# First attention of a fused four-layer block: low parts by offsets, outputs one a step, twelve product buffers

## The chip, the cores and the metric

The program runs on one NeuronCore of one Trainium2 chip. The metric is the device time of one execution in microseconds (us), the median of three runs. TensorE (PE) multiplies matrices, VectorE (DVE) and GpSimd (POOL) work elementwise, ScalarE (ACT) evaluates functions, SyncE (SP) issues the transfers. The engines run their own instruction streams and meet at semaphores.

## The reference, cut to what matters

Eight stages follow each other (four attentions, four feed-forward layers), each of the form `x = x + stage(layernorm(x))` on x of 16 x 64 x 512. The change touches the first attention alone: for each of 8 heads of 8 channels, position t attends to a window of 16 neighbours.

```python
q = _pointwise(Wq, bq, x)
k = jnp.pad(_pointwise(Wk, bk, cond), ...)
v = jnp.pad(_pointwise(Wv, bv, cond), ...)
idx = jnp.arange(T)[:, None] + jnp.arange(W)[None, :]      # W = 16 offsets
dots = jnp.einsum('bhdt,bhdtw->bhtw', qh, k_win) * scale
attn = jax.nn.softmax(dots, axis=-1)
out = jnp.einsum('bhtw,bhdtw->bhdt', attn, v_win)
return _pointwise(Wo, bo, out.reshape(B, C, T))
```

## The kernel before, in words

x is held as eight tiles of 128 x 512 (two batch rows of 64 channels on the partitions, the 512 positions along the row). `attn0` (line 292) returns one function for each engine. Its parts, in order of time:

1. Projections of k, v and q, then the 16 score products, reduced over the channels by PE (line 371) into `dots`, 128 x (16 offsets x 512 positions).
2. Softmax, in four cuts of 128 positions: DVE takes the maximum away (449), ACT exponentiates (531), PE sums the 16 offsets with an identity (376), DVE takes the reciprocal (453) and multiplies (455). The weights are then split into a high part (ACT, 534) and the rest, the low part (DVE `low(c)`, 459), since the next product is done in a rounded float type, once with each part. DVE's order is divide 0, divide 1, low 0, divide 2, low 1, divide 3, low 2, low 3. PE meanwhile issues 22 filler products (`stay_busy`, 378) and waits for all four low parts (380).
3. The loop of 64 steps n: four pairs of tiles (`PAIRS`, p = n // 16), and 16 offsets w in each. A *wide step* (399) is four products on PE: they spread the weights of offset w from 32 rows to the 128 rows of two tiles, high and low part added up in PSUM. The two tiles sit in different row groups, so two of the four run side by side. The spread weights have two places, banks 0-1 and 2-3. DVE multiplies them with the shifted v (483) into one of `SLOTS` = 8 buffers. POOL adds the buffers of two steps (509). PE applies the output matrix to the two summed tiles (`to_out(k)`, 382), two f32 products, each shown as two records, into banks 4-5 or 6-7 by turns of p. It does so after every odd step, from n = 5: two wide steps, then one `to_out` with its two products.
4. When all eight sums of a pair of tiles are in, DVE adds them to x with the bias (472, `add`) and takes the moments of both tiles for the next layernorm (234, 235). It does so after its product of w = 7 of the next pair, for the last pair at the end.

The order of each engine's stream is written by hand; nothing is planned by a program. Waits: wide step n waits for product n-2, that is, for its place; product n waits for wide step n and for its buffer; a sum for its two products; `to_out(k)` for sum k and, on the first of a pair, for the adds that read its banks. The next stage (`ffn0`) starts when the last add is done.

## Time and profile before

| | us |
|---|---|
| median of 3 runs | 1675.38 (1674.85 to 1675.93) |
| profiled execution, its own time | 1682.93 |
| its span | 1681.6 |
| first wide step to last output product | 119.7 to 237.0 |

| engine | busy over the span |
|---|---|
| PE | 95% |
| DVE | 60% |
| POOL | 34% |
| ACT | 28% |

A row of a timeline gives the start, the duration, the engine and line, the operation with what it writes and reads, how many instructions are merged in the row, and in brackets how long the engine had been idle and who released it. A matmul record contains its way through the array, so records overlap and the distance of their starts is the pace. PEld is the weight load that belongs to a matmul. PEclk is the granted clock of TensorE, 1.00 or 0.50 at any moment.

### The profile page before, as it was taken

What the parts mean: (1) busy time and instruction counts of PE and PEld (TensorE: products, weight loads), DVE (VectorE), ACT (ScalarE), POOL (GpSimd) and SP (SyncE); (2) the same over time, 40 slices, a digit from 0 to 9 for tenths busy, and PEclk for the clock granted to TensorE, in tenths of its full rate; (3) what the DMA queues carried; (4) which work ended last, traced back from release to release, by engine and by line L of the source; (5) the groups of instructions that cost most, each with busy time, mean ns of one, the idle gap of its engine ahead of it and who ended that gap; (6) DMA issues with size and microseconds to landing.
All of it is one profiled execution on the core that took longest, in us unless ns stands there. A gap on an engine that the chain in (4) does not pass through costs nothing.

```text
span 1681.6 us, 22246 instructions
## 1 busy us (share of the span) xinstructions
PE 1602.4 (95%) x9380; PEld 1156.9 (69%) x9380; DVE 1003.3 (60%) x1328; ACT 470.8 (28%) x682; POOL 567.4 (34%) x402
## 2 busy tenths in 40 slices
PE   8979989999989999999999999998999999899998
PEld 2264437888658877788787878877755466568786
DVE  5987765223552665564555646554762379786765
ACT  4140012000422334233432323332101456531010
POOL 3907642221244334131432313231132054462211
PEclk9989979999989999999999999999999999999999
DMA  3000032100200211011010110100210121500000
GB/s 127 1 1 0 1 123 79 50 0 32 100 13 0 85 41 63 20 44 38 26 38 26 63 38 26 38 1 1 104 49 1 26 53 28 193 1 13 13 13 13
DMA packets 18019, 66.55 MB, mean 40 GB/s; under 512 B 1440, under 2 KB 9760, under 8 KB 13312
## 3 DMA queue, kind: packets, MB, share of 16 engines
q1 hardware_dynamic: 17920, 65.12, 11.2%
q8 instruction: 75, 1.23, 0.3%
q14 instruction: 24, 0.20, 0.0%
HBM read 58.82 MB, written 2.10 MB: 36 GB/s over the span
## 4 chain that ended last, share of the span: by engine, by line
PE 80%; DVE 12%; ACT 3%; issue 2%; POOL 2%; DMA 1%; SPq 0%; DVEq 0%; ACTq 0%; POOLq 0%
PE banks L270 47%; PE banks L264 27%; PE banks L399 2%; DVE arena L442 2%; PE banks L1913 1%; DVE arena L1434 1%; DVE grouped_split L1466 1%; PE banks L2186 1%; PE banks L1320 1%; DVE arena L234 1%; DVE arena L1421 1%; DVE window L483 1%; ACT arena L1537 1%; ACT arena L1536 1%; POOL up_lo L859 1%
## 5 line engine op out<-in xcount | busy, mean ns | idle before, releaser
L270 PE MATMUL banks<-grouped_split 128*128 128x512 f32 x1536 | 367.4, 395 | 6.8 <-DVE grouped_split L1466 6.1
L270 PEld LDWEIGHTS banks<-grouped_split 128*128 128x128 f32 x1536 | 284.7, 189 | 70.0 <-DVE grouped_split L1466 9.3
L1603 POOL TENSOR_TENSOR arena<-arena,attn_tables 128x512 f32<-128x512 f32 x80 | 102.1, 1281 | 312.7 <-ACT arena L1537 312.7
L270 PE MATMUL banks<-experts_split 128*128 128x512 f32 (+1 forms) x792 | 181.6, 392 | 1.9 <-DVE experts_split L630 1.9
L270 PEld LDWEIGHTS banks<-experts_split 128*128 128x128 f32 (+1 forms) x792 | 146.5, 185 | 36.4 <-issue 2.5
L1421 DVE TENSOR_TENSOR arena<-banks,attn_tables 128x512 f32<-128x512 f32 x80 | 54.7, 684 | 129.9 <-ACT arena L1537 129.9
L264 PE MATMUL banks<-arena 128*128 128x64 f32 (+2 forms) x698 | 111.9, 313 | 14.7 <-DVE arena L1434 6.8
L264 PEld LDWEIGHTS banks<-arena 128*128 128x128 f32 x698 | 96.5, 196 | 36.3 <-issue 27.7
L660 DVE SCALAR_TENSOR_TENSOR arena<-banks,experts,arena 128x512 f32<-128x512 f32 x64 | 47.6, 750 | 106.8 <-PE banks L270 106.8
L1434 DVE TENSOR_TENSOR arena<-arena 128x512 f32<-128x512 f32 x80 | 70.5, 881 | 54.6 <-POOL arena L1603 54.5
L509 POOL TENSOR_TENSOR window<-window 128x1024 f32<-128x1024 f32 x32 | 75.7, 2368 | 73.9 <-DVE window L483 73.9
L1536 ACT ACTIVATE arena<-banks 64x512 f32<-64x512 f32 x80 | 47.7, 596 | 177.4 <-PE banks L270 133.7
L264 PE MATMUL banks<-window,arena 128*128 128x128 f32 (+1 forms) x256 | 88.0, 493 | 6.5 <-ACT window L531 5.7
L483 DVE TENSOR_TENSOR window<-banks,window 128x1024 f32<-128x1024 f32 x64 | 75.2, 1219 | 29.0 <-PE banks L399 29.0
L264 PE MATMUL banks<-dense 128*32 128x64 f32 (+4 forms) x1738 | 84.1, 290 | 5.3 <-ACT dense L2047 3.4
L2416 POOL TENSOR_TENSOR dense<-dense,arena 128x512 f32<-128x512 f32 (+1 forms) x32 | 37.3, 1166 | 136.8 <-DVE dense L2293 136.8
L264 PEld LDWEIGHTS banks<-dense 128*32 128x32 f32 (+3 forms) x1738 | 55.4, 125 | 38.2 <-issue 31.0
L699 POOL TENSOR_TENSOR experts_split<-experts,experts_split 128x2048 fp32r<-128x2048 f32 x8 | 36.8, 4601 | 116.9 <-ACT experts_split L680 116.9
L1473 DVE TENSOR_TENSOR arena<-banks,arena 128x512 f32<-128x512 f32 x64 | 43.0, 681 | 55.0 <-PE banks L270 55.0
L264 PE MATMUL banks<-dense,arena 128*32 128x128 f32 (+1 forms) x640 | 74.3, 340 | 0.0
L264 PEld LDWEIGHTS banks<-window,arena 128*128 128x128 f32 x256 | 40.6, 212 | 38.5 <-issue 30.2
L1608 POOL TENSOR_TENSOR arena<-arena 128x1024 f32<-128x1024 f32 x16 | 30.5, 1904 | 97.0 <-DVE arena L1457 97.0
(289 smaller groups left out, 2961.3 us busy)
## 6 DMA issues: line engine op xcount, KB each, us to landing
grouped<-in_attn SPq DMA_DIRECT2D x16, 1024.0 KB, 5.0
experts<-in_expert SPq DMA_DIRECT2D x8, 1024.0 KB, 4.8
linear<-in_ffn SPq DMA_DIRECT2D x1, 4096.0 KB, 13.3
grouped<-in_attn SPq DMA_DIRECT2D x8, 512.0 KB, 3.6
dense<-arena SPq DMA_DIRECT2D x16, 256.0 KB, 4.3
dense<-in_w SPq DMA_DIRECT2D x1, 3584.0 KB, 12.0
dense<-in_attn SPq DMA_DIRECT2D x1, 3072.0 KB, 13.5
dense<-in_w SPq DMA_DIRECT2D x1, 2688.0 KB, 10.2
```

The source lines that it names most:

```text
L264: return pe.matmul(dst, lhsT=lhsT, rhs=rhs, start=(k == 0), stop=(k == n - 1))
L270: s = pe.matmul(dst, lhsT=lhsT[i], rhs=rhs[j], start=(k == 0 and x == 0), stop=(k == n - 1 and x == 2))
L483: v.tensor_tensor(f(AV + n % SLOTS * 2 * D, 2 * D, 2, D), bank[:, n % 2 * 2:n % 2 * 2 + 2, :], spread(f(V0 + PAIRS[p][0] * KW + w, D), 2, ...
L509: g.tensor_tensor(f(at, 2 * D), f(at, 2 * D), f(at + 2 * D, 2 * D), ALU.add).then_inc(pair_done.sem, 1)
L660: v.scalar_tensor_tensor(x, bank[:, t, :], f(WREP + e * NT + t, 1), x, ALU.mult, ALU.add).then_inc(x_done.sem, 1)
L699: g.tensor_tensor(r(EXS + e % 2 * 2 * LOT + LOT, LOT), f(STAGED + e % 3 * LOT, LOT), r(EXS + e % 2 * 2 * LOT, LOT).bitcast(F32), ALU.subtr ...
L1421: v.tensor_tensor(f(QC + i % 2 * HALF, HALF), bank[:, place(u), :], COS[:, h * HALF:(h + 1) * HALF], ALU.mult).then_inc(bank_v.sem, 1)
L1434: v.tensor_tensor(to, qc, rot, ALU.add).then_inc(rot_add.sem, 1)
L1473: v.tensor_tensor(x, bank[:, place(u), :], x, ALU.add).then_inc(bank_v.sem, 1)
L1536: act.activation(rot[0:64, :], bank[64:P, b, :], ACT.Copy)
L1603: g_.tensor_tensor(rot, rot, SIN[:, h * HALF:(h + 1) * HALF], ALU.mult).then_inc(rot_sin.sem, 1)
L2416: g.tensor_tensor(blocks, blocks, m.const("down32").unsqueeze(1).broadcast_to([P, nb, BLK]), ALU.mult).then_inc(eq_done.sem, 1)
```

## The change

In the stage `attn0` alone:

- The low parts are made by four groups of four offsets (all 512 positions each) after all four divides; ACT makes the high part of the last cut in four pieces. Wide step 0 waits for the first low part, steps 4, 8 and 12 for the next ones. DVE makes low parts 1, 2, 3 after its products 0, 3, 7.
- The filler products go from 22 to 13.
- The spread weights have three places (banks 0-1, 2-3, 6-7), so wide step n waits for product n-3. The output sums of a pair of tiles have two banks (4, 5), the same for every pair of tiles, so the first output product of a pair of tiles waits for the adds of the one before.
- `to_out(k)` is cut into its two products: one after wide step 2k+5 and one after 2k+6, for the first k of a pair of tiles 2k+7 and 2k+8. So none is issued after steps w = 5 and 6 of pairs 1 to 3, and two after w = 7 and 8. Five are left for the end, four before.
- There are twelve buffers for the products (four over k, eight over `dots`); `sizes = (2,) * 8` keeps sums of two steps, 32 of them.
- DVE adds after its product w = 5 instead of 7, and takes the moments of the two tiles after the products w = 7 and 9.

```diff
--- before.py
+++ after.py
@@ -297,7 +297,12 @@
     TOP, PROD = V0 + NT * KW, CT
     DOTS = TOP + D
     ATT = DOTS + WIN * D
-    AV, SLOTS, SUM = DOTS, 8, PROD + 2048
+    SLOTS, SUM = [K0 + j * 2 * D for j in range(4)] + [DOTS + j * 2 * D for j in range(8)], PROD + 2048
+    sizes = (2,) * 8
+    groups = [(p * WIN + sum(sizes[:i]), n) for p in range(4) for i, n in enumerate(sizes)]
+    sums = [(first, pair) for first, size in groups for pair in (((0, 1), (2, 3), (0, 2)) if size == 4 else ((0, 1),))]
+    summed = {first + pair[1]: n for n, (first, pair) in enumerate(sums)}
+    last_sum = {first: n for n, (first, pair) in enumerate(sums)}
     seltr = m.buf("selt_split", CT, NT * P, F32R)
     w0_in, const_in = m.sem("w0_in", 16), m.sem("const_in", 16)
     x_in, c_in = [m.sem(f"x_in{h}", 16) for h in range(2)], [m.sem(f"c_in{h}", 16) for h in range(2)]
@@ -305,9 +310,9 @@
     prod_v, prod_g, dots_mm, dots_out, max_done = (
         m.sem(n, k) for n, k in (("prod_v", 48), ("prod_g", 48), ("dots_mm", 128), ("dots_out", 16), ("max", 16)))
     sub_done, exp_done, sum_mm, sum_done, att_done, hi_done, low_done = (
-        m.sem(n, 4) for n in ("sub", "exp0", "sum_mm", "sum_done", "att", "att_hi", "att_low"))
+        m.sem(n, k) for n, k in (("sub", 4), ("exp0", 4), ("sum_mm", 4), ("sum_done", 4), ("att", 4), ("att_hi", 7), ("att_low", 4)))
     selt_done, wide_mm, av_done, pair_done, out_mm = (
-        m.sem(n, k) for n, k in (("selt_done", 1), ("wide_mm", 64), ("av_done", 64), ("pair_done", 32), ("out0_mm", 32)))
+        m.sem(n, k) for n, k in (("selt_done", 1), ("wide_mm", 64), ("av_done", 64), ("pair_done", len(sums)), ("out0_mm", len(groups))))
     add_done = m.sem("add0_done", NT)
     ON_V, ON_G = ((0, 2), (4, 6), (7,)), (1, 3, 5)
     Q_BANK = {0: 0, 2: 1, 4: 2, 6: 3, 7: 4}
@@ -323,6 +328,7 @@
             place[what, t] = Q_BANK[t]
         else:
             place[what, t], ring = 5 + ring % 3, ring + 1
+    WIDE = (0, 2, 6)
     cuts = [slice(c * P, (c + 1) * P) for c in range(4)]
     scale0 = HD0 ** -0.5
     bias0 = f(W0 + 4 * P, 4)
@@ -375,34 +381,40 @@
             for w in range(WIN):
                 s = mm(pe, bank[:, c, 0:P], m.const("ident"), dots[:, w, cut], w, WIN)
             s.then_inc(sum_mm.sem, 1)
-        stay_busy(m, pe, 7, 22)
+        stay_busy(m, pe, 7, 13)
         pe.wait_ge(*selt_done(1))
-        pe.wait_ge(*low_done(4))
-
-        def to_out(k):
-            p = k // 8
-            pe.wait_ge(*pair_done(k + 1))
-            if k % 8 == 0 and p >= 2:
-                pe.wait_ge(*add_done(2 * (p - 1)))
-            for i in range(2):
-                s = mm(pe, bank[:, 4 + p % 2 * 2 + i, :], f(W0 + 3 * P, P), f(AV + (2 * k % SLOTS * 2 + i) * D, D),
-                       k % 8, 8)
-            s.then_inc(out_mm.sem, 1)
-
+
+        def to_out(k, x):
+            first, size = groups[k]
+            p, i = k // len(sizes), k % len(sizes)
+            pe.wait_ge(*pair_done(last_sum[first] + 1))
+            if i == 0 and p:
+                pe.wait_ge(*add_done(2 * p))
+            s = mm(pe, bank[:, 4 + x, :], f(W0 + 3 * P, P), f(SLOTS[first % 12] + x * D, D), i, len(sizes))
+            if x:
+                s.then_inc(out_mm.sem, 1)
+
+        due = [first + size - 1 + (6 if size == 4 or first % WIN == 0 else 4) for first, size in groups]
         for n in range(4 * WIN):
             p, w = n // WIN, n % WIN
-            if n >= 2:
-                pe.wait_ge(*av_done(n - 1))
+            if n >= 3:
+                pe.wait_ge(*av_done(n - 2))
+            if n % 4 == 0 and p == 0:
+                pe.wait_ge(*low_done(w // 4 + 1))
             for x, part in enumerate((hi, lo)):
                 for i, t in enumerate(PAIRS[p]):
                     rows = slice(t // 2 * 32, t // 2 * 32 + 32)
-                    s = pe.matmul(bank[:, n % 2 * 2 + i, :], lhsT=seltr[rows, t * P:(t + 1) * P], rhs=part[rows, w, :],
+                    s = pe.matmul(bank[:, WIDE[n % 3] + i, :], lhsT=seltr[rows, t * P:(t + 1) * P], rhs=part[rows, w, :],
                                   start=x == 0, stop=x == 1)
             s.then_inc(wide_mm.sem, 1)
-            if n % 2 and n >= 5:
-                to_out((n - 5) // 2)
-        to_out(30)
-        to_out(31)
+            for k in range(len(groups)):
+                for x in range(2):
+                    if due[k] + x == n:
+                        to_out(k, x)
+        for k in range(len(groups)):
+            for x in range(2):
+                if due[k] + x >= 4 * WIN:
+                    to_out(k, x)
 
     def vector(v):
         def scale(t):
@@ -454,37 +466,47 @@
             v.wait_ge(*sum_done(c + 1))
             v.tensor_tensor(dots[:, :, cuts[c]], dots[:, :, cuts[c]], over_w(SUM, cuts[c]), ALU.mult).then_inc(att_done.sem, 1)
 
-        def low(c):
-            v.wait_ge(*hi_done(c + 1))
-            v.tensor_tensor(lo[:, :, cuts[c]], dots[:, :, cuts[c]], hi[:, :, cuts[c]].bitcast(F32),
-                            ALU.subtract).then_inc(low_done.sem, 1)
-
-        divide(0)
-        for c in range(1, 4):
+        def low(j):
+
+            four = slice(4 * j, 4 * j + 4)
+            v.wait_ge(*hi_done(3 + j + 1))
+            v.tensor_tensor(lo[:, four, :], dots[:, four, :], hi[:, four, :].bitcast(F32), ALU.subtract).then_inc(low_done.sem, 1)
+
+        for c in range(4):
             divide(c)
-            low(c - 1)
-        low(3)
+        low(0)
 
         def add(p):
-            v.wait_ge(*out_mm(8 * (p + 1)))
+            v.wait_ge(*out_mm(len(sizes) * (p + 1)))
             for i, t in enumerate(PAIRS[p]):
                 x = f(X + t * D, D)
-                v.scalar_tensor_tensor(x, bank[:, 4 + p % 2 * 2 + i, :], bias0[:, 3:4], x, ALU.add,
+                v.scalar_tensor_tensor(x, bank[:, 4 + i, :], bias0[:, 3:4], x, ALU.add,
                                        ALU.add).then_inc(add_done.sem, 1)
-            for i, t in enumerate(PAIRS[p]):
-                v.wait_ge(*add_done(2 * p + i + 1))
-                m.moments(v, 1, t)
+
+        def moments(p, i):
+            v.wait_ge(*add_done(2 * p + i + 1))
+            m.moments(v, 1, PAIRS[p][i])
 
         for n in range(4 * WIN):
             p, w = n // WIN, n % WIN
             v.wait_ge(*wide_mm(n + 1))
-            if n >= SLOTS:
-                v.wait_ge(*out_mm((n - SLOTS) // 2 + 1))
-            v.tensor_tensor(f(AV + n % SLOTS * 2 * D, 2 * D, 2, D), bank[:, n % 2 * 2:n % 2 * 2 + 2, :],
+            if n - 12 in summed:
+                v.wait_ge(*pair_done(summed[n - 12] + 1))
+            elif n >= 12:
+                v.wait_ge(*out_mm([first for first, size in groups].index(n - 12) + 1))
+            v.tensor_tensor(f(SLOTS[n % 12], 2 * D, 2, D), bank[:, WIDE[n % 3]:WIDE[n % 3] + 2, :],
                             spread(f(V0 + PAIRS[p][0] * KW + w, D), 2, 2 * KW, D), ALU.mult).then_inc(av_done.sem, 1)
-            if w == 7 and p:
+            if n in (0, 3, 7):
+                low({0: 1, 3: 2, 7: 3}[n])
+            if n in (3, 5, 7, 9):
+                v.wait_ge(*low_done((n - 1) // 2))
+            if w == 5 and p:
                 add(p - 1)
+            if w in (7, 9) and p:
+                moments(p - 1, (w - 7) // 2)
         add(3)
+        moments(3, 0)
+        moments(3, 1)
 
     def pool(g):
         g.memset(f(HALVES, NT), -0.5).then_inc(m.half_set.sem, 1)
@@ -503,11 +525,14 @@
                     g.wait_ge(*dots_mm(NT * (w - 1) + TURN.index(t) + 1))
                 g.tensor_tensor(f(PROD + t * D, D), f(XT + t * D, D), f(K0 + t * KW + w, D),
                                 ALU.mult).then_inc(prod_g.sem, 1)
-        for k in range(2 * WIN):
-            at = AV + 2 * k % SLOTS * 2 * D
-            g.wait_ge(*av_done(2 * k + 2))
-            g.tensor_tensor(f(at, 2 * D), f(at, 2 * D), f(at + 2 * D, 2 * D), ALU.add).then_inc(pair_done.sem, 1)
-            if k == 27:
+        for n, (first, (to_step, other_step)) in enumerate(sums):
+            to, other = (f(SLOTS[(first + x) % 12], 2 * D) for x in (to_step, other_step))
+            if (to_step, other_step) == (0, 2):
+                g.wait_ge(*pair_done(n))
+            else:
+                g.wait_ge(*av_done(first + other_step + 1))
+            g.tensor_tensor(to, to, other, ALU.add).then_inc(pair_done.sem, 1)
+            if n == len(sums) - 6:
                 m.rsqrt_half(g, 1, 0)
         m.rsqrt_half(g, 1, 1)
 
@@ -531,7 +556,8 @@
             act.activation(dots[:, :, cut], dots[:, :, cut], ACT.Exp, scale=scale0).then_inc(exp_done.sem, 1)
         for c, cut in enumerate(cuts):
             act.wait_ge(*att_done(c + 1))
-            act.activation(hi[:, :, cut], dots[:, :, cut], ACT.Copy).then_inc(hi_done.sem, 1)
+            for ws in [slice(0, WIN)] if c < 3 else [slice(4 * j, 4 * j + 4) for j in range(4)]:
+                act.activation(hi[:, ws, cut], dots[:, ws, cut], ACT.Copy).then_inc(hi_done.sem, 1)
 
     m.end = add_done(NT)
     return tensor, vector, scalar, pool, sync
```

## Rows read from the trace of the kernel before

**Rows 1.** The page: the chain that ended last, shares of the span by line
```profile
PE banks L270 47%; PE banks L264 27%; PE banks L399 2%; DVE arena L442 2%; PE banks L1913 1%; DVE arena L1434 1%; DVE grouped_split L1466 1%; PE banks L2186 1%; PE banks L1320 1%; DVE arena L234 1%; DVE arena L1421 1%; DVE window L483 1%; ACT arena L1537 1%; ACT arena L1536 1%; POOL up_lo L859 1%
```

**Rows 2.** Timeline, softmax to first wide step (start, us, engine, what, idle before)
```profile
96.77 11.44 PE L264 MATMUL banks<-window,arena 128*128 128x128 f32 x101
...
101.10 0.96 DVE L453 RECIPROCAL arena<-banks 128x128 f32<-128x128 f32 x1 [0.29 <-PE banks L264]
102.10 2.29 DVE L455 TENSOR_TENSOR window<-window,arena 128x2048 f32<-128x2048 f32 x1
...
108.05 9.66 PE L264 MATMUL banks<-arena 128*128 128x256 f32 x44
...
115.10 4.49 DVE L459 TENSOR_TENSOR window_split<-window,window_split 128x2048 fp32r<-128x2048 f32 x2
...
119.73 1.85 PE L399 MATMUL banks<-window_split,selt_split 32*128 32x512 f32 x8 [2.02 <-DVE window_split L459]
```

**Rows 3.** Groups by line, 0 to 260 us: ACT on 512 elements a row
```profile
L527 ACT ACTIVATE window<-banks 128x512 f32<-128x512 f32 x16 | 9.6, 598 | 45.8 <-PE banks L371 45.8
```

**Rows 4.** Timeline, one steady pair of steps and the next one's start
```profile
136.52 1.19 PE L399 MATMUL banks<-window_split,selt_split 32*128 32x512 f32 x8
...
137.29 2.35 DVE L483 TENSOR_TENSOR window<-banks,window 128x1024 f32<-128x1024 f32 x2 [0.69 <-PE banks L399]
...
137.64 1.98 PE L264 MATMUL banks<-window,arena 128*128 128x512 f32 x4
138.18 0.19 PEld L264 LDWEIGHTS banks<-window,arena 128*128 128x128 f32 x1 [0.24 <-issue]
138.61 0.19 PEld L264 LDWEIGHTS banks<-window,arena 128*128 128x128 f32 x1 [0.24 <-issue]
...
139.56 1.20 PE L399 MATMUL banks<-window_split,selt_split 32*128 32x512 f32 x8
```

**Rows 5.** Timeline, first adds and moments amid the loop
```profile
157.83 1.40 DVE L472 SCALAR_TENSOR_TENSOR arena<-banks,arena 128x512 f32<-128x512 f32 x2
...
160.76 4.60 DVE L483 TENSOR_TENSOR window<-banks,window 128x1024 f32<-128x1024 f32 x4
...
162.02 0.73 PE L399 MATMUL banks<-window_split,selt_split 32*128 32x512 f32 x4 [1.07 <-DVE window L483]
...
163.15 0.74 PE L399 MATMUL banks<-window_split,selt_split 32*128 32x512 f32 x4 [0.40 <-DVE window L483]
```

**Rows 6.** Windows: us, busy time of PE, PEld, DVE, ACT, POOL, then PEclk
```profile
119.70:130.30 10.60, 9.91 (x28) 4.27 (x28) 7.08 (x6) 0.00 (x0) 6.74 (x3) 0.52 0.00 0
...
164.40:167.80 3.40, 3.40 (x8) 1.28 (x8) 0.96 (x1) 0.00 (x0) 3.40 (x2) 0.50 0.00 0
...
219.00:229.20 10.20, 10.20 (x20) 3.95 (x20) 4.62 (x4) 0.00 (x0) 6.38 (x3) 0.50 0.01 2
```

**Rows 7.** Timeline, the loop's first outputs and the wide steps behind them
```profile
126.87 3.65 PE L264 MATMUL banks<-window,arena 128*128 128x512 f32 x4
...
130.45 1.18 PE L399 MATMUL banks<-window_split,selt_split 32*128 32x512 f32 x8
```

**Rows 8.** Timeline, a pair of steps at half the clock
```profile
218.96 1.21 PE L399 MATMUL banks<-window_split,selt_split 32*128 32x512 f32 x4 [0.39 <-DVE window L483]
...
220.10 3.78 PE L264 MATMUL banks<-window,arena 128*128 128x512 f32 x4
...
223.81 2.07 PE L399 MATMUL banks<-window_split,selt_split 32*128 32x512 f32 x8
...
225.81 3.67 PE L264 MATMUL banks<-window,arena 128*128 128x512 f32 x4
```

**Rows 9.** Timeline, the last steps and the end of the stage
```profile
229.41 1.20 PE L399 MATMUL banks<-window_split,selt_split 32*128 32x512 f32 x8
...
232.62 2.34 POOL L509 TENSOR_TENSOR window<-window 128x1024 f32<-128x1024 f32 x1 [2.77 <-DVE window L483]
...
235.01 1.98 PE L264 MATMUL banks<-window,arena 128*128 128x512 f32 x4 [0.77 <-POOL window L509]
...
237.04 1.41 DVE L472 SCALAR_TENSOR_TENSOR arena<-banks,arena 128x512 f32<-128x512 f32 x2 [4.50 <-PE banks L264]
```

## The prediction, made before the changed kernel was timed

> **What bounds the kernel now.** I read the page's chain of work first: four fifths of it are matmuls, and no line of the first attention's loop but 399 (2%) and 483 (1%) has a share of its own, the output products being hidden in line 264, which is a helper [rows 1]. So the stage had to be read in its timeline. It runs from 119.73 (first wide step) to 236.99 (last output product, 235.01 + 1.98), 117.3 us [rows 2, 9]. In the steady part two steps take 139.56 - 136.52 = 3.04 us [rows 4]. Who ends last there? DVE is busy 2.35 of the 3.04 and idle 0.69, released by PE; POOL needs 2.34 for its sum [rows 4, 9]. PE's starts follow each other without a gap. Also the next wide step at 139.56 waits for nothing: the product that frees its place began at 137.29 and lasted half of 2.35, so it was done at 138.5. PE is the bound of the loop. The reader should take the distance of starts, not the durations, as PE's price.
>
> Those 3.04 us split. Eight wide matmuls take 1.19, four take 0.73, so a wide step costs 0.46 [rows 4, 5]. Inside the outputs the weight loads start at 138.18 and 138.61, a pass of 0.43; an output product has two passes, 0.86 [rows 4]. Two wide steps and two products are 2 x 0.46 + 4 x 0.43 = 2.64. The other 0.40 is the price of going over from wide steps to outputs and back: the first pass takes 138.18 - 137.64 = 0.54 instead of 0.43, the last from 138.61 + 0.43 = 139.04 to 139.56, 0.52, and the rest falls on the ends of the wide steps. One such *change-over* per pair of steps, 0.40.
>
> The Trainium skill ("TensorE: Matmul & The Clock Gate", "LDWEIGHTS (loading the stationary operand)") gives a load of 128 columns as 128 / 1.2 GHz, which would be an estimated 0.11 for each direction and 0.21 for a change-over, if only the load were exposed. The trace's first pass agrees (0.54 - 0.43 = 0.11), but the whole is 0.40, so the row decides. By the page's figure alone the loss below would be 4.5 instead of 8.4.
>
> The second thing in the loop is the clock. PEclk falls to 0.50 three times after the adds, for 3.4 us each (164.4; one like it at 191.7) and for 10.2 us (219.0), and it is 0.52 in the first 10.6 us of the loop, where PE waits for DVE [rows 6].
>
> **The change part by part.**
>
> *Softmax and start.* The sums of the four cuts end at 108.21, some 3.5 apart (96.77 + 11.44) [rows 2]; the third is in at 104.7. Without the low parts between them the divides are 0.96 + 2.29 = 3.25 each [rows 2]: the third runs 104.7 to 107.95, the fourth waits for its sum and runs 108.25 to 111.5. Then a quarter of ACT's high part: 512 elements a row, 0.60 [rows 3], done 112.1. Low part 0 has the old size, 4.49 / 2 = 2.25 [rows 2], 112.2 to 114.45. First wide step at 114.6 instead of 119.73: **5.1 gained**. The filler has 13 of 22 products, 9.66 x 13 / 22 = 5.7 from 108.05, ends 113.8 and is no hindrance [rows 2].
>
> *Low parts inside the loop.* They don't vanish: three of 2.25 go between DVE's products. Wide step 7 waits for product 4 (three places), so DVE does five products of 4.60 / 4 = 1.15 [rows 5] and two low parts: 114.6 + 0.77 (137.29 - 136.52, wide step to product [rows 4]) + 5.75 + 4.5 = 125.6. In that time PE stands still most of the time, as it did before, so I take half the clock. Wide step 7 at half clock is 220.10 - 218.96 = 1.14 [rows 8], and it is followed by two output products, 130.45 - 126.87 = 3.6 [rows 7]. So step 8 starts at 130.5. Before, step 6 started at 130.45 with the same two outputs done [rows 7]. Of the 5.1 only two wide steps, 0.9, are left at this point: PE's products are late, not the softmax. This is the wait that is late next.
>
> *Outputs one a step.* Now every step has its change-over. Before there were 32 `to_out`, the last two together: 31 of them. After the change outputs follow 57 - 6 = 51 steps (n = 7 to 63 without the two of each later pair). 20 to 21 more x 0.40 = **8.4 lost**. Cover that would hide it: none, PE is the bound. DVE's product waits less for PE, but it had 0.69 to spare already. A step is 0.46 + 0.86 + 0.40 = 1.72 at full clock, 3.44 for two against 3.04.
>
> *Third place, two output banks, earlier adds.* After w = 5 of a later pair DVE adds (1.40 [rows 5]). Count from wide step w = 4: it and one output take 1.7; steps 5, 6, 7 follow without outputs to 3.3; product 5 starts at 1.7 + 0.77, ends 3.6, the adds end at 5.0. The output behind step 7 waits for them, since its bank is theirs: PE is idle from 3.3 to 5.1. Queued behind it on PE is everything, the next wide step too. Then come two outputs, step 8, two outputs (9.6), step 9 and one output (11.3). Six steps of 1.72 would be 10.3: each of three places costs 1.0, in all 3. Before, the stop was 1.07 + 0.40 [rows 5]; the third place doesn't save it, since the new bank wait is longer than the old place wait.
>
> *Moments* are two times about 0.8 on DVE, which then has 0.5 of spare a step: nothing. *Twelve buffers*: product n needs the buffer of n - 12, whose output follows step n - 6 or n - 4: no wait, nothing. The additional semaphore waits on DVE lie in the same spare time. POOL's 32 sums of 2.34 fit in 3.44: nothing.
>
> *The clock after the stops.* All three stops before were followed by a fall to 0.50. The new ones are 1.8 us in one piece, with three wide steps ahead of them, so I expect falls again. What one costs: a fall of 3.4 us costs 1.7, one of 10.2 costs 5.1 [rows 6]; at the good end zero, if none comes. How soon the clock rises matters: at 219.0 it stayed low over an output row, two wide steps (223.81, 2.07) and rose only behind the next output row (225.81, 3.67) [rows 8]. After a new stop outputs come as two, one wide step, two: more output passes in a row than elsewhere, so mostly a short fall, sometimes a longer one. I take 2.3 each, 6.8 in all, nearer to the short rows.
>
> *Sum.* Step 8 starts 130.5. It has two outputs: 0.46 + 1.72 + 0.40 = 2.6, to 133.1. Steps 9 to 62: 54 x 1.72 = 92.9, three stops 3.1, the clock 6.8: step 63 starts at 235.9. The end: product 63 after 0.77 + 1.15, the sum 2.34, the last two outputs 1.98 [rows 9], with handovers 6.4: 242.3. The five outputs left over lie before that sum is done. Before: 236.99. So **5.3 slower**. As a ledger: the loop's PE work was 64 x 0.46 + 128 x 0.43 + 31 x 0.40 = 96.9 of 117.3, and becomes 105 of 127.7. Adds, moments and the next stage follow as before (237.04 [rows 9]). The profiled execution's own 1682.93 becomes 1688.2; it lies 7.5 over the median, which I take for both kernels: 1675.38 + 5.3 = **1680.7**.
>
> **The rivals.**
>
> *No falls* (the clock holds through the stops, because three wide steps run ahead of them): 6.8 less, 1673.9. For it: PE is idle only about 1.8 a place. Against: before, it fell after shorter stops each time. This is the rival of the other side: its place is the 1.8 us before the output behind w = 7, its price 2.3 each, and it decides from two of three falls missing (-4.6, which makes the sum +0.7).
>
> *Cheap change-overs*: if an output after a single wide step does not pay 0.40 (say the 0.40 comes from four passes in a row and not from the change of shape), 8.4 go: 1672.3. For it: nothing in the trace shows single outputs between single wide steps. Against: the 0.54 and 0.52 stand right at the borders of the outputs.
>
> *The clock stays low*: in a half-clock stretch one output per step gives at most two output passes in a row, and where two wide steps lay beside the outputs the clock did not rise [rows 8]. If it isn't raised at the two double outputs behind a stop, it stays until the next ones, 12 steps later. A half-clock step costs 1.14 [rows 8] and two passes of twice 0.43, with some 0.2 at the border of the output, in all 3.05, which is 1.33 more than 1.72: 12 x 1.33 = 16 for one such place, 1697.
>
> *Start not earlier* (high part by pieces or PE's sums late): the loop's pace of DVE sets step 8, so 2 more at most.
>
> **How the numbers follow.** Forecast (1677 to 1685) 0.47; no falls 0.15; cheap change-overs 0.15, half of it together with fewer falls (down to 1666); low clock over a stretch 0.15; rest 0.08 spread about. Later stages have falls of their own, whose places can shift with the stage's end: +-1.7 or two times that. The range takes in the lower rivals but for 0.08 and the low stretch once: 1671 to 1697. What a measurement of this kernel can tell from no change is 0.2%, 3.4 us. Slower by more needs 1678.7: most of the forecast and the low stretch, 0.53. Within: no falls, part of the forecast, part of the cheap case, 0.29. Faster by more: under 1672.0, 0.18.
>
> **What would show it.** First wide step near 114.6; step 8 near 130.5. Two steady steps at 3.44: at 3.04 the change-over step is wrong. An idle PE of 1.8 before the second outputs of pairs 1 to 3, released by the adds. PEclk 0.50 behind each: if it stays 1.00, the no-falls rival holds; if 0.50 lasts over 10 us, the other. Last output product near 242. Wrong altogether if DVE is without idle time in the steady part, since then PE isn't the bound I take it for.

## The result, and the profile after

The changed kernel takes 1690.48 us (median of 5, 1686.74 to 1694.67) against 1675.89 (1674.85 to 1676.17): ratio 1.0086, 95% interval 1.0064 to 1.0108. It is slower by 14.6 us, where 5.3 was forecast. The profiled execution's own time went from 1682.93 to 1694.18, its span from 1681.6 to 1692.9. The ratios, here and below, weigh all executions of both kernels and not the medians alone, so they need not be the quotient of the medians.

First the softmax and the start of the loop, in the timeline of after. It answers to [rows 2] and [rows 7]; L407 is the wide step, L497 the product, L473 a low part, L483 the add.

```profile
112.53 2.29 DVE L473 TENSOR_TENSOR window_split<-window,window_split 128x2048 fp32r<-128x2048 f32 x1 [0.69 <-ACT window_split L560]
...
114.97 1.66 PE L407 MATMUL banks<-window_split,selt_split 32*128 32x512 f32 x12 [0.84 <-DVE window_split L473]
...
120.34 3.48 PE L407 MATMUL banks<-window_split,selt_split 32*128 32x512 f32 x12 [2.60 <-DVE window L497]
...
126.08 1.22 PE L407 MATMUL banks<-window_split,selt_split 32*128 32x512 f32 x4 [2.26 <-DVE window L497]
...
127.23 3.54 PE L264 MATMUL banks<-window,arena 128*128 128x512 f32 x4
...
130.70 0.73 PE L407 MATMUL banks<-window_split,selt_split 32*128 32x512 f32 x4
```

The first wide step starts at 114.97 (forecast 114.6), step 7 at 126.08, step 8 at 130.70 (forecast 130.5). The two idle times of 2.60 and 2.26, released by VectorE's products, are the low parts in the loop: there the 4.8 us won at the start are spent.

The steady part of after, answering to [rows 4]:

```profile
152.19 0.73 PE L407 MATMUL banks<-window_split,selt_split 32*128 32x512 f32 x4
152.84 1.12 PE L264 MATMUL banks<-window,arena 128*128 128x512 f32 x2
153.90 1.66 PE L407 MATMUL banks<-window_split,selt_split 32*128 32x512 f32 x12
```

From 152.19 to 153.90 one step takes 1.71; it was 1.52. The x12 row is steps w = 5, 6 and 7 without outputs. Behind it, answering to [rows 5], the same timeline has the stop:

```profile
155.81 1.40 DVE L483 SCALAR_TENSOR_TENSOR arena<-banks,arena 128x512 f32<-128x512 f32 x2
...
157.35 3.41 PE L264 MATMUL banks<-window,arena 128*128 128x512 f32 x4 [1.79 <-DVE arena L483]
```

The wait is 1.79, forecast 1.8, released by the adds. The windows of after hold the clock's falls that bear on the sum (PE, PEld, DVE, ACT, POOL busy, PEclk), answering to [rows 6]:

```profile
157.70:161.10 3.40, 3.40 (x6) 1.08 (x6) 2.55 (x4) 0.00 (x0) 2.18 (x2) 0.50 0.02 5
188.40:195.20 6.80, 6.80 (x11) 2.01 (x9) 3.28 (x5) 0.00 (x0) 2.48 (x2) 0.50 0.00 0
219.10:222.50 3.40, 3.15 (x4) 1.17 (x4) 3.15 (x5) 0.00 (x0) 3.15 (x3) 0.51 0.00 0
1222.70:1236.30 13.60, 13.60 (x55) 11.87 (x54) 2.54 (x6) 0.63 (x1) 0.00 (x0) 0.50 0.33 137
1458.20:1461.60 3.40, 3.19 (x92) 3.10 (x96) 0.00 (x0) 0.16 (x1) 0.00 (x0) 0.50 0.02 5
```

Three falls behind the three stops, 13.6 us in all, so 6.8 us lost, as put into the sum (TensorE is busy in nearly all of this time, so half of it is lost). The stage's end, answering to [rows 9]:

```profile
236.38 5.79 PE L264 MATMUL banks<-window,arena 128*128 128x512 f32 x12
```
```profile
242.21 1.41 DVE L483 SCALAR_TENSOR_TENSOR arena<-banks,arena 128x512 f32<-128x512 f32 x2 [4.50 <-PE banks L264]
```

The last output product ends at 242.17, forecast 242.3; the adds start at 242.21 instead of 237.04 [rows 9], 5.2 later. Below, *the adds' start* is this mark.

The rest of the difference lies elsewhere. The last two windows are falls that the profile of before has not. This is the place of the first of them in ffn2, eight transposes and the product that waits for ScalarE's copy of them, first before, then after:

```profile
1213.03 3.66 PE L283 MATMUL banks<-arena,dense 128*128 128x128 f32 x32
1217.81 7.36 PE L264 MATMUL banks<-arena 128*128 128x64 f32 x64 [1.12 <-ACT arena L1763]
```
```profile
1216.17 3.66 PE L283 MATMUL banks<-arena,dense 128*128 128x128 f32 x32
1220.94 12.38 PE L264 MATMUL banks<-arena 128*128 128x64 f32 x64 [1.12 <-ACT arena L1789]
```

The same work and the same stop of 1.12 us; the clock held in one and fell in the other, and 7.36 became 12.38. Setting the same VectorE instructions of both traces side by side gives the ledger of the 11.3 between the two spans: first attention +5.2, the next stage -2.0, ffn2 +6.5, the fall at 1458 +1.6.

Is the clock also behind the loss of the executions that were not profiled? Each has its span and its mean granted clock on record. The span times one less the clock is the time that a clock below 1.00 takes away, if TensorE is busy meanwhile, as it is for 95% of the span. For the changed kernel's five executions the mean clock is 0.976 to 0.983 and this time is 33.5 us on average; for 23 executions of the kernel before, timed beside the first experiments, it is 0.980 to 0.988 and 24.3 us. So by this estimate some 9 us of the 14.6 are the clock's, and the rest is work and waits. Where in these executions the clock fell, it does not say.

### The profile page after: what moved, and what is told of

Read it like the earlier page. It is cut to its first block, busy times and chain, and to the rows that moved or that the text cites. A ratio compares the mean times of both kernels' runs of the same rounds, so it can differ in the third digit from the quotient of the medians.

```text
span 1692.9 us, 22220 instructions
## 1 busy us (share of the span) xinstructions
PE 1608.9 (95%) x9362; PEld 1154.1 (68%) x9362; DVE 1006.9 (59%) x1328; ACT 470.6 (28%) x685; POOL 571.1 (34%) x402
## 4 chain that ended last, share of the span: by engine, by line
PE 82%; DVE 11%; ACT 3%; issue 2%; POOL 2%; DMA 0%; SPq 0%; DVEq 0%; ACTq 0%
PE banks L270 46%; PE banks L264 30%; PE banks L407 2%; DVE arena L454 2%; PE banks L1939 1%; DVE arena L1460 1%; DVE grouped_split L1492 1%; PE banks L2212 1%; PE banks L1346 1%; DVE arena L1447 1%; ACT arena L1563 1%; ACT arena L1562 1%; POOL up_lo L885 1%; POOL down_lo L885 1%; DVE window L432 1%
## 5 line engine op out<-in xcount | busy, mean ns | idle before, releaser
L534 POOL TENSOR_TENSOR window<-window 128x1024 f32<-128x1024 f32 x32 | 79.6, 2492 | 74.7 <-DVE window L497 74.6
L264 PE MATMUL banks<-window,arena 128*128 128x128 f32 (+1 forms) x256 | 92.7, 497 | 11.2 <-ACT window L556 5.7
L497 DVE TENSOR_TENSOR window<-banks,window 128x1024 f32<-128x1024 f32 x64 | 77.2, 1220 | 29.0 <-PE banks L407 29.0
## 6 DMA issues: line engine op xcount, KB each, us to landing
dense<-in_w SPq DMA_DIRECT2D x1, 3584.0 KB, 12.2
dense<-in_attn SPq DMA_DIRECT2D x1, 3072.0 KB, 13.6
```

Source lines behind the costliest of these rows:

```text
L264: return pe.matmul(dst, lhsT=lhsT, rhs=rhs, start=(k == 0), stop=(k == n - 1))
L497: v.tensor_tensor(f(SLOTS[n % 12], 2 * D, 2, D), bank[:, WIDE[n % 3]:WIDE[n % 3] + 2, :], spread(f(V0 + PAIRS[p][0] * KW + w, D), 2, 2 * K ...
L534: g.tensor_tensor(to, to, other, ALU.add).then_inc(pair_done.sem, 1)
```

## The experiments

Every kernel was timed beside the kernel before, 5 to 12 executions each. *The lost clock* below is the estimate of the result section, averaged over a kernel's executions. Where an expectation names the "first adds" with a time, it counts from the first moments, 1.3 us behind the adds' start (243.5 for 242.21).

**How far does the kernel before repeat?** No edit.

> The kernel before, unchanged, to see how far its own executions and its falls of the clock repeat. My theory: in the stages behind the first attention a fall of the granted clock depends on how short waits of TensorE happen to lie, so a profiled execution can have one more or one less and moves by 1.7 us for each 3.4 us at half clock. Then the profile of this run has its span within 3 us of 1681.6 or near 1675, and the places of the falls behind 260 us are the same but for one or two. Rival: the falls are fixed by the program; then the span is 1681.6 within 0.5 and all falls stand at the same times. Timed ratio 1.000 in both.

Median 1676.54 (ratio 1.0016, interval 0.9995 to 1.0036). The span of its profile is 1675.3, 6.3 below that of the front section. Its adds start earlier:

```profile
234.08 1.41 DVE L472 SCALAR_TENSOR_TENSOR arena<-banks,arena 128x512 f32<-128x512 f32 x2 [4.50 <-PE banks L264]
```

That is 3.0 before the 237.04 of [rows 9]: two falls in the loop (6.8 and 3.4 us) instead of three (3.4, 3.4, 10.2), so one of its three stops brought none. Behind 260 us the falls stand at the same places, and 6.8 us less of them. So the theory holds: the places are those of the program, the falls do not all repeat. The profile that the prediction stood on had more of them than usual; all executions of this kernel in the study range from 1673.4 to 1690.6, with 72 of 103 at 1674 to 1677.2. The slow ones have the lower clock: 0.976 at 1690.55, 0.988 at 1674.38. A third profile of the same first attention (in the run with fillers in ffn2) has 233.87.

**Both products of a sum behind one step again.**

```diff
-                    if due[k] + x == n:
+                    if due[k] == n:
...
-                if due[k] + x >= 4 * WIN:
+                if due[k] >= 4 * WIN:
```

> The changed kernel with one edit: both output products of a sum are issued behind the same wide step (2k+5, or 2k+7), as before the change. Theory (each going over from wide steps to outputs and back costs 0.40 us): some 20 change-overs fewer, 8 us less in the loop, two steady steps at 3.04 instead of 3.44 us, last output product near 234 us, time some 8 us under the changed kernel's, 1682, and as the start is 5 us earlier than before, no more than 2 us under or over the kernel before in the first attention. Rival (it is the three places with two output banks, or the low parts in the loop, that cost): two steps at 3.04 but the stage's end within 2 us of the changed kernel's 242.

Two steady steps take 3.04 again, and the adds start at 234.91, 7.3 before the changed kernel's. The change-over is the cost it was taken for (8 expected). The expectation's count was short, though: output products now follow 26 of the 64 steps and not 51, since the first two sums of each pair of tiles come together behind w = 7. That is 25 change-overs or 10.0 us. Some of it comes back: a wait of 0.38 ahead of each stop, and 0.77 for the last sum, 1.9 in all. Behind that of the start the falls in the loop are as long as in the changed kernel (13.6 us).

Median 1685.13, ratio 1.0038 (1.0021 to 1.0055). Of the 14.6 us, 5.4 went by the medians, 8.0 by the ratios, and 6.8 between the two profiled executions. The rest stays, and so does the clock's part: the lost clock is 34.4 us, against 33.5, and its profile, too, has the fall of 13.7 us in ffn2.

```profile
138.58 1.19 PE L407 MATMUL banks<-window_split,selt_split 32*128 32x512 f32 x8
139.71 1.98 PE L264 MATMUL banks<-window,arena 128*128 128x512 f32 x4
141.62 1.20 PE L407 MATMUL banks<-window_split,selt_split 32*128 32x512 f32 x8
```

**Single products alone, in the kernel before.**

```diff
-            if n % 2 and n >= 5:
-                to_out((n - 5) // 2)
+            if n >= 5:
+                to_out((n - 5) // 2, ((n - 5) % 2,))
+        to_out(29, (1,))
```

> The kernel before with one edit: its two output products go behind two successive wide steps, one each (behind step 2k+5 and 2k+6). Banks, places, buffers, low parts and adds as before. Theory: 58 change-overs instead of 31, 27 x 0.40 = 10.8 us more, two steady steps at 3.44 us, last output product near 248 us. Rival (the change-over is not what costs in the changed kernel): the loop stays within 2 us of 237.

Median 1764.01, ratio 1.0523 (1.0494 to 1.0552): 88 us, not 11. In the windows of its profile the clock is down for the whole loop:

```profile
122.10:313.20 191.10, 190.52 (x367) 61.25 (x366) 84.59 (x82) 0.00 (x0) 76.33 (x33) 0.50 0.00 0
313.20:318.00 4.80, 3.39 (x8) 1.14 (x6) 1.37 (x3) 0.00 (x0) 0.00 (x0) 0.99 0.00 0
```

and in its timeline each step takes 3.15 (129.41 to 132.56), although TensorE is never idle:

```profile
129.41 2.07 PE L264 MATMUL banks<-window,arena 128*128 128x512 f32 x2
131.41 1.22 PE L401 MATMUL banks<-window_split,selt_split 32*128 32x512 f32 x4
132.56 2.08 PE L264 MATMUL banks<-window,arena 128*128 128x512 f32 x2
```

It fell while the first wide steps ran at VectorE's pace, and with one wide step and one output product by turns it did not rise again before the six products in a row at the end (from 309.14). This is the prediction's rival of a clock that stays low, at more than five times its price (88 against 16). The 10.8 us of the expectation cannot be read from this run.

The changed kernel may escape it by a detail: the two double outputs behind w = 7 and 8, which came in only because one pair of banks has to wait for the adds. Its clock rose there each time, but no run takes only these away, so the detail is argued and not shown.

**A plain delay ahead of the loop.**

```diff
         pe.wait_ge(*low_done(4))
+        stay_busy(m, pe, 7, 24)
```

> The kernel before with 24 filler products more on TensorE, issued when all low parts are done, ahead of the first wide step: 24 x 0.22 = 5.3 us of delay and nothing else. Theory A (the part of the loss behind the first attention comes from the later stages lying otherwise against the clock's changes): the times are more than 5.3 us up and spread over several us from run to run, as those of the changed kernel do (1686.7 to 1694.7), with falls behind 1200 us that the kernel before has not. Theory B (the later loss belongs to the changed kernel's own edits, or to chance of one execution): the time is 5.3 us up within 1, to 1681, and spreads by 1.3 us as before.

The expectation mis-sized the delay: a filler product is two records of 0.22, and part ran at half clock.

```profile
119.75 12.29 PE L264 MATMUL banks<-arena 128*128 128x256 f32 x48 [2.02 <-DVE window_split L460]
131.96 1.20 PE L400 MATMUL banks<-window_split,selt_split 32*128 32x512 f32 x8
```

So the loop starts 12.2 later. The median is 1696.04 (1689.9 to 1697.3), ratio 1.0102 (1.0078 to 1.0127), 20 above that of before: 8 more than the delay. In its profile falls stand in the loop at other places (137.1, 178.1 and 205.4, for 10.2, 3.4 and 10.2 us) and two later that before has not (1451.2, 1512.7), but none in ffn2. This is for theory A, with the delay corrected: a delay by itself moves the time by more than itself and spreads it. The lost clock is 29.4 us against 24.3; a part of these 5 lies in the fillers themselves, but most of the 8 is the clock's by this estimate.

**Is the fall in ffn2 the later loss?**

```diff
+        stay_busy(m, pe, 6, 5)
         pe.wait_ge(*m.xt_done(24 + NT))
```

> The changed kernel with five filler products (5 x 0.22 = 1.1 us) in the feed-forward layer of the third block (ffn2), behind its eight transposes, where TensorE otherwise stands still for 1.12 us both before and after the change. In the changed kernel's profile the clock fell there at 1222.7 for 13.7 us; in the kernel before the same stop with the same length stands at 1216.7 and the clock held. Theory (the loss behind the first attention is this fall, met by the stage's new time and not by any edit): no fall there, some 6.5 us less than the changed kernel, 1684. Rival (the later loss comes from something else that the change brings): the time stays at 1690.

> The kernel before with the same five filler products in ffn2. Both theories expect little: the clock held at this place in two of two profiles of it, so its median stays within 1 us of 1676. Should the fall be frequent in executions that were not profiled (those of 1680 to 1685), the slow ones become rarer.

Five products are 2.2 us, not 1.1, so some 1.1 is the filler's own price. In the changed kernel no fall remains there:

```profile
1218.74 9.41 PE L264 MATMUL banks<-arena 128*128 128x256 f32 x74
```

These are ten filler records and the 64 that took 12.38. The span went from 1692.9 to 1684.2, the highest execution from 1694.7 to 1688.4, the median only to 1687.62 (ratio 1.0062, 1.0040 to 1.0084). In the kernel before: 1676.93, ratio 1.0001 (0.9986 to 1.0016), no change. The cause is right for the profiled executions, but the expected 1684 was not reached. In the median the fall accounts for 2.9 us, or 4 with the filler's own price, and the lost clock came down by just that, from 33.5 to 29.5. The first attention leaves some 6.5 of the 14.6 us unexplained (14.6 less the 8.1 by which its adds start later than 234.08).

**The start alone, and the places alone.** The first keeps low parts, filler and buffers of the change and goes back in the rest (`WIDE = (0, 2)`, banks `4 + p % 2 * 2 + x`, outputs whole behind 2k+5, adds and moments at w = 7). The second is the kernel before with what the first leaves out, but for the single outputs: three places, two output banks, the adds after w = 5, the moments after w = 7 and 9. The outputs stay whole, and those of w = 5 come behind w = 7 with its own.

> The changed kernel with the loop's banks, places, output order and adds put back to those of before; left of the change are the low parts by offsets, the shorter filler and the twelve buffers. Theory: the first wide step comes 5 us earlier, at 115, but the loop has its three low parts to make, so that step 8 starts about when it did before (133.5), within 1.5 us; the end of the stage is 0 to 3 us earlier than before (237.0). Rival (the earlier start is kept): last output product at 232.

> The kernel before with three places for the spread weights, two banks for the output sums, the adds after w = 5 and the moments after w = 7 and 9; low parts, filler, eight buffers and paired outputs as before. Theory: each of three stops of TensorE becomes one piece of 1.8 us before the outputs behind w = 7 (before: 1.07 + 0.40), and four output products follow in a row, so that the clock is up again at once; two steady steps stay at 3.04; last output product within 3 us of 237. Rival (the third place is a gain that the single outputs have hidden): stops of under 1 us, end at 232 or earlier.

The start alone: adds at 230.32, 3.8 before the 234.08. That is more than the expected 0 to 3, and step 8 comes 3.0 earlier than before (133.48), where it was expected at about the same time; the expectation was wrong about where the start's gain goes. In its timeline the first outputs follow step 5, at 124.00, and not step 7, at 127.23:

```profile
122.85 1.22 PE L407 MATMUL banks<-window_split,selt_split 32*128 32x512 f32 x4 [0.19 <-DVE window L497]
124.00 3.48 PE L264 MATMUL banks<-window,arena 128*128 128x512 f32 x4
```

Step 8 comes at 130.45 with four output products done, where the changed kernel has two at 130.70. The run with the outputs together shows the price of holding them back: it, too, waits until step 7 with the first, and reaches step 8 with four products done 2.1 later.

```profile
127.18 5.41 PE L264 MATMUL banks<-window,arena 128*128 128x512 f32 x8
132.51 1.18 PE L407 MATMUL banks<-window_split,selt_split 32*128 32x512 f32 x8
```

Median 1677.01, ratio 1.0008 (0.9988 to 1.0028): no difference in time that can be told. The lost clock is 28.0 us against 24.6 of the kernel before beside it, so by this estimate the clock took back, over all its executions, about what the start gives.

The places alone: adds at 236.90, 2.8 later than 234.08. Its stops are one piece of 1.80, preceded by 0.38, with a fall behind each (6.8, 3.4, 6.8 us), and it has the 13.7 us in ffn2. Median 1682.30, ratio 1.0030 (1.0010 to 1.0050). These falls are 17.0 us against 10.2 in the kernel before again, and half of the difference, 3.4, is more than the 2.8: by themselves the places cost nothing. The rival, a hidden gain that would show in the time, is out.

```profile
153.16 0.74 PE L400 MATMUL banks<-window_split,selt_split 32*128 32x512 f32 x4 [0.38 <-DVE window L488]
155.69 6.63 PE L264 MATMUL banks<-window,arena 128*128 128x512 f32 x8 [1.80 <-DVE arena L476]
```

**The stops filled.** In the kernel before (w = 10) and in the changed kernel (w = 7):

```diff
+            if w == 10 and p:
+                pe.wait_ge(*add_done(2 * p))
+                stay_busy(m, pe, 4 + (p - 1) % 2 * 2, 2)
```
```diff
+                        if p and w == 7 and k % 8 == 0:
+                            pe.wait_ge(*av_done(n - 1))
+                            stay_busy(m, pe, WIDE[(n + 1) % 3], 4)
```

> The kernel before with two filler products (0.88 us) on TensorE in each of its three stops behind the adds (ahead of wide step w = 10 of pairs 1 to 3, where it waits 1.07 to 1.28 us for VectorE). Theory (a stop costs far more through the clock than by its own length): no fall at the three places, so 5 us less in the first attention than in a profile of before with three falls, 2 to 4 less than in the better ones, first adds of the end near 232 instead of 235 to 238; median 1672. Rival (the falls come from the wide steps that have only 32 rows each, not from the stops): falls as before, time 1675 to 1676.

> The changed kernel with four filler products (1.76 us) on TensorE in each of its three stops of 1.79 us, ahead of the output products behind w = 7, into the bank pair of the next wide step. It measures the term of the prediction that was put at 6.8 us (three falls at 2.3). Theory: no falls near 158, 188 and 219, the first attention ends 6.8 us earlier than in the changed kernel (first adds near 236.7 instead of 243.5), and the timed median comes down by as much or more, to 1683 or less, as the next weak places are met at other times. Rival (the falls come from one output product a step, not from the stops): falls in the loop as before and the end stays at 243; or, as in the kernel with single products only, a low clock for a long stretch.

In both profiles there is no fall in the loop behind that of its start. Before: the adds start at 229.30, 4.8 ahead of 234.08. After: at 236.29, 5.9 ahead of 242.21, where the term was put at 6.8. In the changed kernel the stop is filled but for 0.39 and the output that waits for the adds is not late:

```profile
155.46 1.99 PE L264 MATMUL banks<-arena 128*128 128x256 f32 x8 [0.39 <-DVE window L500]
157.29 1.88 PE L264 MATMUL banks<-window,arena 128*128 128x512 f32 x4
```

The falls belong to the stops, and one product a step at full clock does not bring it down. In the medians little of it arrives, and the expected 1672 and 1683 are both missed: 1675.55 (ratio 1.0003, 0.9988 to 1.0019; executions from 1672.0 to 1680.9) and 1686.47 (ratio 1.0066, 1.0040 to 1.0092; from 1680.5 to 1691.4). The profiled executions have spans of 1671.8 and 1682.1, at the lower ends of these.

In the kernel before the lost clock is 24.2 us with the fillers and 23.7 without: over all executions nothing was won, though the profile has no fall at the stops. In the changed kernel it is 28.4 against 33.5. Its six executions fall into two groups, 1680.5 to 1683.4 at a clock of 0.985 to 0.987 and 1689.6 to 1691.4 at 0.980 and 0.981. The profile is of the first group; what fell in the second, no trace shows.

**A version that beats both, and one that does not.** The first is the start alone with the fillers at w = 10 and `stay_busy(m, pe, 6, 2)` in ffn2; the second has `sizes = (2, 2, 2, 4, 2, 2, 2)` on top.

> The part of the change that gains by itself (low parts by offsets, 13 fillers, twelve buffers; two places, paired outputs and double output banks as before) with the same fillers in the three stops, and two fillers (0.88 us) in the 1.12 us stop of ffn2. Theory: both gains add up, end of the first attention 3 to 4 us under the low-parts-only kernel's 231.6 on this mark, no fall near 1210; median 1670. Rival (what is gained there is given back by falls later): median 1675.

> As the kernel just before, and one of the sums of each pair of tiles is over four steps instead of two: seven output sums instead of eight, so 4 x 2 output products and 4 change-overs fewer, (4 x 1.71 + 4 x 0.40) = 8.4 us of TensorE less; GpSimd has nine additions of 2.37 instead of eight, 21.3 us of some 23. Theory A (TensorE is the bound, its work counts): 4 to 8 us less than the kernel before this one. Theory B (two steps without outputs, at VectorE's pace, bring the clock down): falls in the middle of each pair of tiles, and no gain or a loss.

The first takes 1672.34 us (1669.96 to 1673.46), ratio 0.9974 (0.9961 to 0.9986), the adds start at 227.47, and it has the narrowest spread of the kernels with twelve executions (3.5 us). The second has one output sum in eight less and takes 1684.48, ratio 1.0052 (1.0034 to 1.0069): theory B. It has less work and the most lost clock of all but the run with single products alone, 39.6 us against 22.0. Its profile has four wide steps at VectorE's pace in each pair of tiles and a fall of 6.8 us in each, the first at 137.4:

```profile
134.04 0.73 PE L410 MATMUL banks<-window_split,selt_split 32*128 32x512 f32 x4 [0.42 <-DVE window L500]
135.17 0.74 PE L410 MATMUL banks<-window_split,selt_split 32*128 32x512 f32 x4 [0.40 <-DVE window L500]
136.30 0.73 PE L410 MATMUL banks<-window_split,selt_split 32*128 32x512 f32 x4 [0.39 <-DVE window L500]
137.43 2.35 PE L410 MATMUL banks<-window_split,selt_split 32*128 32x512 f32 x8 [0.40 <-DVE window L500]
```

## Why the prediction was right, and where it was not

- The time lies above the forecast's 1677 to 1685. It lies in the whole range only because that reaches to 1697 for a low stretch that this kernel did not have, so that the range held is luck. The sum for the first attention is not luck: its steps came out one by one.
- *TensorE bounds the loop, a step becomes 1.72*: right, 1.71. The 20 to 21 more change-overs were put at 8.4; undoing 25 gave 7.3, with 1.9 of waits that come with the undoing. The Trainium skill ("TensorE: Matmul & The Clock Gate", "The mechanism") says that a weight load overlaps running matmuls only if the row groups differ; an output's load covers all of them, and the first output pass after a wide step is indeed longer, 0.54 against 0.43 [rows 4]. The whole 0.40 is more than such a load, and no run shows what the rest is.
- *The start*: 114.97 against 114.6, step 8 at 130.70 against 130.5 (the terms given for it add up to 130.3). The reading that only 0.9 of it is left because the products are late holds for this order. The start alone keeps 3.0 of it; holding the first outputs back to step 7 cost 2.1 (132.51 against 130.45).
- *The stop*: 1.79 against 1.8. *The clock behind the stops*: 6.8 against 6.8 in the profile, 5.9 when taken away. *The end of the loop*: 242.17 against 242.3.
- *No falls* and *cheap change-overs* are refuted. The argument against the first, that it fell after shorter stops "each time", was that of one profile: in the kernel before again and in the start alone one stop in three brought no fall. *The clock stays low* was not what this kernel did, but the run with single products alone shows it real and priced too low: 16 us was one stretch of 12 steps, and there it lasted through the loop. A step took 3.15 where 3.05 was put.
- What failed is "it lies 7.5 over the median, which I take for both kernels". That put an error of the two profiles' places straight into the forecast. The profile of before had more falls in the first attention than two others of the same stage; measured from 234.08 the adds start 8.1 later, not 5.2. For after the profile lies 3.7 over the median.
- And the term for later stages, "+-1.7 or two times that", was too small: +8.1 (6.5 in ffn2 and 1.6 at 1458) and -2.0 in the profile. The sum then closes: 5.2 + 6.1 for the profiles, + 7.0 - 3.7 for where these lie over their medians (1682.93 - 1675.89, 1694.18 - 1690.48), 14.6.

The parts add up on the marks of the profiles: 234.08, the start -3.8, places, bank waits and later first outputs +4.6 (234.91 - 230.32), single products +7.3, in all 242.2. They do so by construction, each being the difference of two profiles, and the clock is in them. Between the start and the adds the falls are 10.2 us in the kernel before again, 6.8 in the start alone, and 13.6 in the outputs together and in the changed kernel. At half of that, 1.7 of the -3.8 and 3.4 of the +4.6 are the clock's, and the 7.3 is free of it.

What stays open: why the clock falls in ffn2 in the profiles of the changed kernel, of the outputs together, of the places alone and of the single products, and in none of the others that have the bare stop (before twice, the delay, the start alone, and both kernels with their stops in the loop filled). The stop is equal in all. That it depends on the moment at which the stage begins fits, but no run set that moment by itself; the delay of 12.2 us did not bring the fall. For the executions that were not profiled the record shows how much clock they lost, not where.

## What to carry to other kernels

When TensorE is the bound, count how often its stream changes from one shape of product to another: each going over and back cost 0.40 us here, a quarter of a step, and interleaving more finely pays that price for nothing if the consumers already have slack. Price a stop of TensorE with what the clock does behind it: in these profiles 1 to 2 us of idleness cost nothing, or another 1.7 to 6.5 us, and a few small fillers in the stop took it away there. Whether that gains time only the executions as a whole tell: the kernel before with its stops filled was no faster. And look at more than one profile of the kernel before: one execution's falls are a sample, here 3 us in one stage and 6 in the whole.

## What the runs showed of the hardware that I had not expected

- The clock can stay at 0.50 for 191 us with TensorE busy all the time (190.52 of 191.10), when short products with 32 rows and single output products alternate. In the changed kernel the same mix, reached at full clock, keeps 1.00 (steps of 1.71 from 133.28 to 153.90).
- A stop of the same length (1.12 us) at the same place of the program, behind the same work, brought the clock down in the profiles of four programs and not in those of five others (before included), and cost 6.5 us in the changed kernel.
- A delay of 12.2 us ahead of the loop cost 20.
- Filling the stops took the falls out of the profile of the kernel before and left the lost clock of its twelve executions where it was (24.2 us, 23.7 without).
